# The second block's down projection in split float32r, with one of six activation chunks kept in X and the response norm in the same stage

## The reference, cut to what matters

```python
y = conv_depthwise_7x7(x) + dw_b                      # x is kept as the identity
y = layernorm(y) * ln_w + ln_b                        # over the 192 channels
y = gelu(y @ w1 + b1)                                 # 192 -> 768
gx = sqrt(sum(y * y, over all pixels of an image))    # 768 numbers per image
nx = gx / (mean(gx over the 768) + 1e-6)
y = grn_gamma * (y * nx) + grn_beta + y
out = x + y @ w2 + b2                                 # 768 -> 192
```

## Time and profile before

| | |
|---|---|
| median of 3 runs | 3580.73 us (3580.53 to 3581.01) |
| the profiled execution | 3581.64 us, its span 3579.5 us |
| TensorE busy | 3423.4 us (96%) |
| VectorE, ScalarE, GpSimd busy | 67%, 50%, 30% |
| the down projection's matmuls | 2814.4 to 3199.8 us of the span, 385.4 us busy |
| DMA | 554.97 MB, 155 GB/s in the mean |

### The profile page before, as it was taken

How to read it: one execution, slowest core, us unless ns; L and a number is a source line. 1 busy time by engine, 2 the same in 40 slices (tenths; PEclk the granted TensorE clock), 3 DMA queues, 4 the chain that set the end, 5 groups by cost and what they waited for, 6 DMA issues and landing times. The chain is left out here.

```text
span 3579.5 us, 95798 instructions
## 1 busy us (share of the span) xinstructions
PE 3423.4 (96%) x31958; PEld 3312.3 (93%) x31958; DVE 2389.3 (67%) x5936; ACT 1790.2 (50%) x5312; POOL 1080.1 (30%) x1951
## 2 busy tenths in 40 slices
PE   7999999999799999999969969989999899989999
PEld 6888888888699999999969969989999899989999
DVE  5777777777556666666659979979999311125554
ACT  4666666666444444444426657659999200002222
POOL 3233333333244444444425520014444223320000
PEclk9999999999899999999989989999999899999999
DMA  1455566610011111111158865537777788877775
GB/s 34 123 197 192 198 239 235 233 58 23 23 34 51 51 51 51 50 51 51 50 141 256 247 188 198 196 124 201 198 198 199 221 253 253 251 228 228 227 227 174
DMA packets 472671, 554.97 MB, mean 155 GB/s; under 512 B 78259, under 2 KB 331957, under 8 KB 472373
## 3 DMA queue, kind: packets, MB, share of 16 engines
q1 hardware_dynamic: 447028, 531.65, 49.3%
q10 hardware_dynamic: 25344, 19.27, 1.7%
HBM read 392.56 MB, written 271.52 MB: 186 GB/s over the span
## 5 line engine op out<-in xcount | busy, mean ns | idle before, releaser
L1325 PE MATMUL PS<-dw_grid,dw_mats 128*128 128x196 f32 (+1 forms) x3840 | 624.0, 326 | 37.0 <-DVE dw_mats L1266 37.0
L1325 PEld LDWEIGHTS PS<-dw_grid,dw_mats 128*128 128x128 f32 x3840 | 623.5, 191 | 37.5 <-DVE dw_grid L1262 37.5
L1297 ACT ACTIVATE dw_res<-PS,dw_brow 128x196 f32<-128x196 f32 x192 | 81.5, 424 | 699.3 <-PE PS L1325 699.3
L981 PE MATMUL PS<-mlp_w,mlp_hid 128*128 128x192 f32 x2352 | 414.0, 326 | 0.5 <-ACT mlp_hid L796 0.5
L1262 DVE COPY dw_grid<-X 32x392 f32 (+3 forms) x480 | 290.3, 605 | 171.8 <-PE PS L1325 148.7
L1560 PE MATMUL PS<-gain,down_hid 128*128 128x192 f32 x2352 | 385.4, 328 | 3.6 <-DMA down_hid<-scratch_hid 3.6
L1560 PEld LDWEIGHTS PS<-gain,down_hid 128*128 128x128 f32 x2352 | 385.1, 191 | 3.9 <-DMA down_hid<-scratch_hid 3.9
L981 PEld LDWEIGHTS PS<-mlp_w,mlp_hid 128*128 128x128 f32 x2352 | 378.3, 190 | 0.8 <-ACT mlp_hid L796 0.8
L796 ACT ACTIVATE mlp_hid<-PS,mlp_b 128x256 f32<-128x256 f32 x588 | 247.0, 471 | 110.8 <-PE PS L787 110.8
L1187 PE MATMUL PS<-sobel_wf,sobel_edge 96*128 96x192 f32 (+1 forms) x1568 | 261.0, 328 | 29.2 <-DVE sobel_edge L1122 28.9
L1187 PEld LDWEIGHTS PS<-sobel_wf,sobel_edge 96*128 96x128 f32 (+1 forms) x1568 | 257.3, 191 | 32.9 <-issue 32.8
(11 more groups left out here) (217 smaller groups left out, 9284.2 us busy)
## 6 DMA issues: line engine op xcount, KB each, us to landing
scratch_hid<-hid_hid SPq DMA_DIRECT2D x196, 384.0 KB, 3.7
down_hid<-scratch_hid SPq DMA_DIRECT2D x196, 384.0 KB, 4.0
scratch_wide<-scratch_taps SPq DMA_DIRECT2D x64, 960.0 KB, 5.3
dw_raw<-scratch_wide SPq DMA_DIRECT2D x96, 640.0 KB, 4.3
scratch_wide<-scratch_taps SPq DMA_DIRECT2D x64, 768.0 KB, 4.7
dw_raw<-scratch_wide SPq DMA_DIRECT2D x96, 512.0 KB, 3.3
sobel_xv<-scratch_v SPq DMA_DIRECT2D x56, 420.0 KB, 5.0
scratch_u<-mlp_u SPq DMA_DIRECT2D x56, 378.0 KB, 3.0
```

What stands on the lines that cost most here:

```text
L981: last = nc.tensor.matmul(psD[i], hid[:, p.buf(2), m, i * 128:(i + 1) * 128], w2[:, m, :], start=(m == 0), stop=(m == MC - 1))
L1325: last = nc.tensor.matmul(dst[:, :, ys, :], m, src, start=(i == 0), stop=(i == len(steps) - 1))
```

## The change

Three things are changed together.

The down projection is computed in float32r with both operands split. ScalarE writes the high part of a block's activations (a copy rounded to float32r), VectorE the low part, the difference, of five chunks, and GpSimd that of the sixth. The gain is split in the same way, and high and low gain lie side by side, so that per chunk there are two matmuls: the high activations against 384 columns (high and low gain), and the low activations against the 192 columns of the high gain, accumulated onto the first half. Both halves are added up by VectorE in two operations (`part`, then X). The parts h_hi and h_lo have two buffers.

The sixth chunk of the hidden activations is no longer stored and loaded: GELU writes it into X itself, whose 192 columns per block are free by then, and the ring and the DRAM buffer hold five chunks. The rings of the down projection are five deep instead of seven.

`response_norm` is no stage of its own any more; its operations stand ahead of the block loop in `project`. The gain of the second image is made by VectorE in front of block 8. The loop is written out for all 196 blocks instead of being a loop on the engines.

```diff
@@ class NormUp
-    def gelu(self, act, pair, hid):
+    def gelu(self, act, pair, place):
...
-                last = nc.scalar.activation(hid[:, m, :], self.psU[i][:, e * 256:(e + 1) * 256], ACT.Gelu, bias=self.b1[:, m:m + 1])
+                last = nc.scalar.activation(place(m), self.psU[i][:, e * 256:(e + 1) * 256], ACT.Gelu, bias=self.b1[:, m:m + 1])
@@ def hidden
+    KEPT = MC - 1
+    hid = s.sb("hid", [128, HR, KEPT, 256])
+    def place(p, m):
+        return hid[:, p.buf(HR), m, :] if m < KEPT else X[:, bass.ds(p.n * 2, 2), 0:128]
@@ def project
+    R, BANKS, LAG = 5, 6, 2
+    KEPT = MC - 1
+    gain = s.sb("gain", [128, IMG, MC, 2, C], F32R)
+    hid = s.sb("hid", [128, R, KEPT, 128])
+    hi, lo = s.parts("h", [128, 2, MC, 128])
...
+            def body(b):
+                if b.reached(R):
+                    sp.wait_ge(q["low"], b.n - R + 1)
+                sp.dma_start(hid[:, b.buf(R)], d["hid"][b.n]).then_inc(hloaded[b.buf(R)], 16)
+                if b.reached(R):
+                    sp.wait_ge(q["out"], b.n - R + 1)
+                sp.dma_start(x2[:, b.buf(R), :], d["x2"][b.n]).then_inc(xloaded[b.buf(R)], 16)
...
+            pool.wait_ge(g["cvec"], 1)
+            def body(b):
+                pool.wait_ge(q["high"], b.n + 1)
+                if b.reached(2):
+                    pool.wait_ge(q["down"], b.n - 1)
+                nc.gpsimd.tensor_tensor(lo[:, b.buf(2), KEPT, :], X[:, b.n, 0:128], as_f32(hi[:, b.buf(2), KEPT, :]), ALU.subtract).then_inc(q["low_kept"], 1)
+                pool.wait_ge(xloaded[b.buf(R)], b.turn(R) * 16 + 16)
+                nc.gpsimd.tensor_tensor(x2[:, b.buf(R), :], x2[:, b.buf(R), :], cvec[:, :], ALU.add).then_inc(q["resid"], 1)
...
+            def body(b):
+                act.wait_ge(hloaded[b.buf(R)], b.turn(R) * 16 + 16)
+                if b.reached(2):
+                    act.wait_ge(q["down"], b.n - 1)
+                nc.scalar.activation(hi[:, b.buf(2), 0:KEPT, :], hid[:, b.buf(R)], ACT.Identity)
+                nc.scalar.activation(hi[:, b.buf(2), KEPT, :], X[:, b.n, 0:128], ACT.Identity).then_inc(q["high"], 1)
...
+            def gains(i):
+                nc.vector.tensor_tensor(gain[:, i, :, 0, :], w2[:, :, :], view(scale[:, i, 0:1], [[1, MC], [0, C]]), ALU.mult).then_inc(g["gain_high"], 1)
+                dve.wait_ge(g["gain_high"], i + 1)
+                for m in range(MC):
+                    last = nc.vector.scalar_tensor_tensor(gain[:, i, m, 1, :], w2[:, m, :], scale[:, i, m:m + 1], as_f32(gain[:, i, m, 0, :]),
+                                                          ALU.mult, ALU.subtract)
+                last.then_inc(g["gain"], 1)
...
+            def body(t):
+                b = t
+                if b.n == 8:
+                    gains(1)
+                if b.inside(NB):
+                    dve.wait_ge(q["high"], b.n + 1)
+                    if b.reached(2):
+                        dve.wait_ge(q["down"], b.n - 1)
+                    nc.vector.tensor_tensor(lo[:, b.buf(2), 0:KEPT, :], hid[:, b.buf(R)], as_f32(hi[:, b.buf(2), 0:KEPT, :]), ALU.subtract).then_inc(q["low"], 1)
+                b = t.back(LAG)
+                if b.inside(NB):
+                    dve.wait_ge(q["resid"], b.n + 1)
+                    dve.wait_ge(q["down"], b.n + 1)
+                    nc.vector.tensor_tensor(part[:, b.buf(2), :], ps(b, 0), x2[:, b.buf(R), :], ALU.add).then_inc(q["part"], 1)
+                    dve.wait_ge(q["part"], b.n + 1)
+                    nc.vector.tensor_tensor(X[:, b.n, :], ps(b, 1), part[:, b.buf(2), :], ALU.add).then_inc(q["out"], 1)
...
-                    for m in range(MC):
-                        last = nc.tensor.matmul(PS[:, b.buf(R), 0:C], hid[:, b.buf(R), m, :], gain2[:, img, m, :], start=(m == 0), stop=(m == MC - 1))
+                pe.wait_ge(g["gain"], img + 1)
+                pe.wait_ge(q["low"], b.n + 1)
+                pe.wait_ge(q["low_kept"], b.n + 1)
+                if b.reached(BANKS):
+                    pe.wait_ge(q["out"], b.n - BANKS + 1)
+                both = PS[:, 2 + b.buf(BANKS), 0:2 * C]
+                for m in range(MC):
+                    nc.tensor.matmul(both, hi[:, b.buf(2), m, :], gain[:, img, m, :, :].rearrange("p e c -> p (e c)"), start=(m == 0), stop=False)
+                    last = nc.tensor.matmul(ps(b, 0), lo[:, b.buf(2), m, :], gain[:, img, m, 0, :], start=False, stop=(m == MC - 1))
+                last.then_inc(q["down"], 1)
+            unrolled(NB, 0, body)
```

More of the change, by code:

```diff
@@ L1342, in hidden, with two @@
     BY_ACT = 2
+    def place(p, m):
+        return hid[:, p.buf(HR), m, :] if m < KEPT else X[:, bass.ds(p.n * 2, 2), 0:128]
+    def two(m):
+        ap = squares[:, m, :]
+        return ap if m < KEPT else ap.rearrange("p (b t) -> p b t", b=2)
     with nc.Block() as block:
@@ L1460, in response_norm, with ps @@
     scale = s.sb("scale", [128, IMG, MC])
+    cvec = s.sb("cvec", [128, C])
+    gain = s.sb("gain", [128, IMG, MC, 2, C], F32R)
+    hid = s.sb("hid", [128, R, KEPT, 128])
+    hi, lo = s.parts("h", [128, 2, MC, 128])
+    x2 = s.sb("x2", [128, R, C])
+    part = s.sb("part", [128, 2, C])
     psM = PS[:, 0, 0:IMG * MC]
     psC = PS[:, 1, 0:C]
-    g = {x: s.sem(x) for x in ("loaded", "ready", "tot", "gx", "sums", "chain", "beta", "const")}
+    g = {x: s.sem(x) for x in ("loaded", "ready", "tot", "gx", "sums", "chain", "beta", "const", "cvec", "gain_high", "gain")}
+    hloaded, xloaded = s.sems("hloaded", R), s.sems("xloaded", R)
+    q = {x: s.sem(x) for x in ("high", "low", "low_kept", "resid", "down", "part", "out")}
+    def ps(b, half):
+        return PS[:, 2 + b.buf(BANKS), half * C:half * C + C]
     with nc.Block() as block:
@@ L1478, in _ @@
             nc.gpsimd.tensor_tensor(gx[:, :, :], tot[:, :, :], phalf[:, :, :], ALU.pow).then_inc(g["gx"], 1)
[L1480 to L1485, removed]
-            for m in range(MC):
-                last = nc.tensor.matmul(psC, beta[:, m, :], w2[:, m, :], start=(m == 0), stop=(m == MC - 1))
-            last.then_inc(g["const"], 1)
+            pool.wait_ge(g["cvec"], 1)
[6 more added lines that the diff above has]
+                nc.gpsimd.tensor_tensor(x2[:, b.buf(R), :], x2[:, b.buf(R), :], cvec[:, :], ALU.add).then_inc(q["resid"], 1)
+            unrolled(NB, 0, body)
+        @block.scalar
+        def _(act):
+            def body(b):
[4 more added lines that the diff above has]
+                nc.scalar.activation(hi[:, b.buf(2), KEPT, :], X[:, b.n, 0:128], ACT.Identity).then_inc(q["high"], 1)
+            unrolled(NB, 0, body)
         @block.vector
@@ L1551, in _ @@
+            unrolled(NB, LAG, body)
         @block.tensor
         def _(pe):
[L1553 to L1562 removed]
+            pe.wait_ge(g["gx"], 1)
@@ new lines, in _, with body @@
+            nc.tensor.matmul(psM, ones[:, :], gx[:, :, :].rearrange("p i m -> p (i m)"), start=True, stop=True).then_inc(g["sums"], 1)
+            pe.wait_ge(g["loaded"], 64)
+            pe.wait_ge(g["beta"], 1)
+            for m in range(MC):
+                last = nc.tensor.matmul(psC, beta[:, m, :], w2[:, m, :], start=(m == 0), stop=(m == MC - 1))
+            last.then_inc(g["const"], 1)
+            def body(b):
+                img = b.n // PER
+                pe.wait_ge(g["gain"], img + 1)
[4 more added lines that the diff above has]
+                both = PS[:, 2 + b.buf(BANKS), 0:2 * C]
+                for m in range(MC):
+                    nc.tensor.matmul(both, hi[:, b.buf(2), m, :], gain[:, img, m, :, :].rearrange("p e c -> p (e c)"), start=(m == 0), stop=False)
+                    last = nc.tensor.matmul(ps(b, 0), lo[:, b.buf(2), m, :], gain[:, img, m, 0, :], start=False, stop=(m == MC - 1))
+                last.then_inc(q["down"], 1)
```

76 lines of the change are left out of this document (15 added, 61 removed).

## The result

The changed kernel takes **3633.04 us** (median of 4 runs, 3631.17 to 3634.08) against 3580.87 for the kernel before on the same chip: a ratio of 1.0142, interval 1.0127 to 1.0157. It is slower by 52 us. I had forecast slower, at 3600 and at most 3622: the direction was right, the size was not.

The account below looks back on a forecast made before the run. TensorE, 96% busy, bounds the kernel before; after the change a two-block loop was to. Terms +17.3 (loop), +3.1 (gains), -2.0 (start), +0.4 (end) gave +18.8 on 3581.64, predicted as 3600 us; range 3568 to 3622.

Parts of the forecast that it names:

- The loop over two blocks: Down projection: with two part buffers, end of b-2, high, low, matmuls of b set the period; 2.04 us a block, +17.3 us.
- The collision: Low parts: GpSimd's subtraction meets VectorE's two-input one and ends 0.32 us behind it; bounds 0 and 0.456.
- Rival 1: Low parts of GpSimd and VectorE do not collide: 1.88 us a block, 3568-3570 us, faster; chance 0.13.
- the sum of 4.065: Two-block loop in us: 0.04 + 0.905 + 0.05 + 0.805 + 0.32 + 0.05 + 1.895, or 2.03 a block.
- Hand-over 0.05: Two-block loop: 0.05 us from the end of the low parts to TensorE's first matmul.
- more waits per instruction than before: TensorE's first matmul of a block has three or four waits: 0 to 0.05 us per loop, without a row.
- TensorE's block: Two-block loop: TensorE's matmuls of one block, first start to last end, 1.895 us, with 0.275 a chunk.
- One sign that I had named as showing me wrong: TensorE, down projection: a 384-column matmul further than 0.175 us from its successor would show the forecast wrong.
- Second image's gains: VectorE makes them in front of block 8's low part: +3.1 us, bounds +2 and +3.5.
- Start and end: Down projection: earlier start, -2.0 us at the end of block 1; two additions behind the last matmul, +0.4.
- Loads: Five-deep load ring: 7.1 us needed against four periods, 8.2; it fits, with 1.1 in hand, 0 us.
- rival 4: The load ring binds: landings of 5.5 us give 2.14 a block and 3620, of 6.2 give 2.31 and 3650; chance 0.10.

Follow-up runs that it names:

- e4: The changed kernel with three buffers instead of two for the high parts, the low parts keeping two: 3549.45 us, ratio to before 0.9913.
- e2: The changed kernel without GpSimd's low part of the sixth, kept chunk in all blocks but the first two: 3585.74 us, ratio to before 1.0019.
- e1: The changed kernel with TensorE's gain wait only in blocks 0 and 98 and the low-part waits last: 3616.51 us, ratio to before 1.0103.
- e6: The changed kernel with the same four TensorE waits per block, gain and output first, low parts last: 3619.28 us, ratio to before 1.0115.
- e3: The changed kernel with the kept chunk's low part made by VectorE instead of GpSimd: 3613.75 us, ratio to before 1.0089.

## Why the prediction was wrong

The mechanism was right, its size was not: +18.8 us forecast, +49.9 in the profiled spans and 52 in the medians.

- **The loop over two blocks**: right, and shown by e4, which took nothing away but ScalarE's link in the loop and won 81 us of the stage.
- **The collision**: right. GpSimd's part took 1.10 us (0.805 + 0.32 worked out), 0.46 alone. The figure had a copy of the MLP stage as its only witness. It agrees with the Trainium skill (GPSIMD Engine Reference, Key points): contention of GpSimd with VectorE's instructions of two SBUF inputs. For these subtractions the rows show a full wait, not a slowing: whether VectorE's work lasts 0.82 or 1.55 us, GpSimd ends 0.3 us behind its end.
- **Rival 1** (3568, no collision) did not come about; and even e2, which took the operation away altogether, is 18 us above it. By e2's rows the loop without GpSimd is 0.10 + 0.93 + 0.04 + 0.83 + 0.10 + 1.92 = 3.92 us, where rival 1 had 3.76: it left out what the hand-overs cost there too.
- **The step that failed**: the hand-overs in the sum of 4.065. "Hand-over 0.05" from GpSimd to TensorE measured 0.26; TensorE to ScalarE 0.10 instead of 0.04; ScalarE to GpSimd 0.08 instead of 0.05. The 0 to 0.05 that I put for "more waits per instruction than before" was the guess that mattered: the order of the waits alone is 0.12 (e1, e6). The rest of the 0.21, 0.09, was not traced to a cause, and neither was why the same order costs nothing like it where the late wait is VectorE's (0.10 in all, in e2 and e3). Together with 0.025 each for the high part and TensorE's block, less 0.03 for the low part, the loop is 4.39 instead of 4.065 to 4.08: 0.15 a block over the 2.04 that I took, **+29 us**.
- **TensorE's block**: 1.92 against a forecast of 1.895; a pair of matmuls 0.283 instead of 0.275. One sign that I had named as showing me wrong did come: in turn a 384-column matmul starts its successor 0.19 to 0.20 us later, further than 0.175. It did little harm, since the short matmul behind it took 0.09 instead of 0.11. The bare formula of the Trainium skill (TensorE: Matmul & The Clock Gate, Back-to-back issue gap) gives 0.245 us a pair, as an estimate, and that does not fit the measured 0.283. The figures of the same section of the Trainium skill for streams that also load weights lie above that formula at 128 columns but below it at 512, so they did not side with a higher value for 384 columns, as my forecast had it.
- **Second image's gains**: 4.7 instead of 3.1. Six operations took 3.01 us there and 2.06 at the start of the stage (the same form); I had 2.14 for both. The trace has three GpSimd operations beside the six, each of them with two inputs in SBUF:

```profile
2829.91 0.71 POOL L1521 TENSOR_TENSOR down_x<-down_x,down_cvec 128x192 f32<-128x192 f32 x1
...
2831.33 0.47 POOL L1519 TENSOR_TENSOR down_h_lo<-X,down_h_hi 128x128 fp32r<-128x128 f32 x1 [0.71 <-ACT down_h_hi L1531]
2831.76 0.70 POOL L1521 TENSOR_TENSOR down_x<-down_x,down_cvec 128x192 f32<-128x192 f32 x1
```

  While GpSimd stood idle, from 2830.75 to 2831.33, VectorE's operations started 0.33 us apart as at the start of the stage; beside either addition one held the next for 0.66 us, and beside the subtraction for 0.53. Here it was VectorE that paid: GpSimd's 128 columns took 0.47.
- **Start and end**: -0.4 together against -1.6. The first two blocks took 8.3 us, from TensorE's first matmul at 2811.01 to the output at 2819.30, where 6.3 had been put.
- **Loads**: right that the ring does not bind; ScalarE waited for TensorE, not for DMA. The landing was 3.2 us instead of 4.0.
- 29 + 1.6 + 1.2 = 32, on 18.8, is the stage's 50.8. My range ended at 3622 because I gave the period of my own case only 2.11 at most, and took in only the near end of rival 4: 0.07 over a sum of seven pieces, three of which were hand-overs, two of them without a row of the same kind. A loop's price is multiplied by 97 here, so 0.3 us in it was worth more than every other term.

## What to carry to other kernels

Before adding engines to the path in front of a saturated one, add up the loop that the buffers close (release, each engine's part, each hand-over, the bound engine's own block) and divide by the number of buffers; if that is above the busiest engine's work, look for one more buffer first: here it gave 81 us of the stage, and leaving GpSimd's operation out altogether only 44. Try the wait that comes last behind all others: it took nothing away from the program and gave 10 to 11 us behind GpSimd's signal, though behind VectorE's (e2, e3) there was no such delay to win. Whether a small operation belongs on GpSimd depends on that loop: inside it GpSimd's subtraction, with the collision and the later hand-over, cost 17 us more than doing it on VectorE, outside it the same offload gained 9.

## What the runs showed of the hardware that I had not expected

- A GpSimd subtraction of 128 columns from SBUF that starts behind VectorE's subtraction of two SBUF tiles stands still until that one ends: 0.46, 1.10 and 1.70 us beside none, one and two of them. VectorE's own 640 columns hardly pay (825 ns mean, 0.81 us at block 8 with GpSimd idle). It goes the other way round too: VectorE's 128 columns took 0.52 instead of 0.28 us behind an addition of GpSimd's in e3, and its gain operations stood up to 0.66 apart instead of 0.33 at block 8, where GpSimd's subtraction took 0.47. So the order and the kind of the operations decide which engine pays.
- TensorE's first matmul starts 0.26 us behind GpSimd's end with one satisfied wait behind the late one, and 0.14 with the same wait ahead of it (e1, e6). Behind VectorE's end it starts after 0.10 us even with satisfied waits behind the late one (e2, e3). What makes the difference was not tried.
- Float32r matmuls of 384 and 192 columns take 0.283 us a pair, in turn or grouped, where one float32 matmul of 192 columns takes 0.328. So the split form, at three products per value, is a seventh cheaper on TensorE, but only if everything in front of it keeps up.
- The second image's gains took 0.5 us per operation in the loop and 0.34 ahead of it; the operations of GpSimd beside them account for it by the rows above, but no run left them all out.
